# One group of 512-column products per piece of probabilities in an attention stage

## The reference

```python
q = heads(xn @ Wq + bq); k = heads(xn @ Wk + bk); v = heads(xn @ Wv + bv)
q = apply_rope(q); k = apply_rope(k)
scores = jnp.einsum('bhid,bhjd->bhij', q, k) / jnp.sqrt(jnp.float32(D_HEAD))
scores = scores * mask + (1.0 - mask) * -1000000000.0      # mask: lower triangle
probs = jax.nn.softmax(scores, axis=-1)
out = jnp.einsum('bhij,bhjd->bhid', probs, v)
```

## Time and profile before

| | |
|---|---|
| median of timed runs | 3622.78 us |
| profiled execution, span of all instructions | 3621.2 us |
| `phase2`, first weighted sum to last | 835 to 2786 us |
| TensorE busy, whole span | 3255.9 us (90%) |
| VectorE / ScalarE / GpSimd busy | 2606.9 / 1734.9 / 928.2 us |
| TensorE idle ahead of each pass of the loop | 2.99 us |
| L1048 (weighted sum), instructions | 11264, 772.9 us busy |
| L1020 (products for exp) | 3072, 905.5 us busy |
| L1003 (products for max) | 3072, 937.9 us busy |

### The profile page before, as it was taken

How to read it: one execution, slowest core, us unless ns; L and a number is a source line. 1 busy time by engine, 2 the same in 40 slices (tenths; PEclk the granted TensorE clock), 3 DMA queues, 4 the chain that set the end, 5 groups by cost and what they waited for, 6 DMA issues and landing times. The chain is left out here.

```text
span 3621.2 us, 79826 instructions
## 1 busy us (share of the span) xinstructions
PE 3255.9 (90%) x22839; PEld 1559.7 (43%) x22839; DVE 2606.9 (72%) x7405; ACT 1734.9 (48%) x3559; POOL 928.2 (26%) x1205
## 2 busy tenths in 40 slices
PE   2888888859999999999999999999998998499999
PEld 1444444413333333333333333333333776265788
DVE  5999999958888888888888888888882555300232
ACT  1444444415767666766766676667666111011000
POOL 4888877721111111111111111111111000201000
PEclk7999989968999999999999999999999999699999
DMA  2566566582434334444344343334442665412000
GB/s 91 156 186 176 171 180 191 167 181 50 95 83 95 80 87 91 91 91 91 91 91 87 85 92 85 82 87 91 91 91 86 232 256 214 150 63 88 3 11 11
DMA packets 173071, 401.91 MB, mean 111 GB/s; under 512 B 34141, under 2 KB 84611, under 8 KB 155927
## 3 DMA queue, kind: packets, MB, share of 16 engines
q1 hardware_dynamic: 152664, 358.73, 37.6%
q10 hardware_dynamic: 18432, 33.56, 2.9%
q0 software_dynamic: 1536, 4.33, 0.4%
HBM read 239.61 MB, written 156.98 MB: 110 GB/s over the span
## 5 line engine op out<-in xcount | busy, mean ns | idle before, releaser
L969 ACT ACTIVATE prob<-ps 128x512 f32<-128x512 f32 (+1 forms) x2560 | 1282.1, 553 | 673.9 <-PE ps L1020 655.0
L892 DVE CUSTOM_DVE_ANT_0 junk<-ps,mask 128x128 bf16<-128x128 f32 (+3 forms) x2048 | 942.5, 486 | 305.5 <-PE ps L1003 285.7
L1003 PE MATMUL ps<-k_rows,q_rows 96*128 96x512 bf16 (+3 forms) x3072 | 937.9, 337 | 78.5 <-DVE mx L892 37.2
L1020 PE MATMUL ps<-q_rows,k_rows 99*128 99x512 bf16 (+3 forms) x3072 | 905.5, 335 | 42.1 <-issue 38.2
L1048 PE MATMUL ps<-prob,v_rows 128*32 128x256 f32 (+1 forms) x11264 | 772.9, 355 | 0.0
L871 POOL TENSOR_SCALAR_AFFINE_SELECT prob<-prob 128x512 f32<-128x512 f32 x512 | 321.8, 640 | 1684.4 <-ACT prob L969 1684.2
L889 DVE TENSOR_REDUCE mx<-ps 128x1 f32<-128x512 f32 x1024 | 687.1, 686 | 41.1 <-PE ps L1003 28.9
L1020 PEld LDWEIGHTS ps<-q_rows,k_rows 99*128 99x128 bf16 x3072 | 275.1, 98 | 600.1 <-ACT prob L969 354.1
L687 PE MATMUL ps<-w_all,x_t 128*128 128x512 f32 (+1 forms) x1024 | 428.6, 543 | 0.0
L1048 PEld LDWEIGHTS ps<-prob,v_rows 128*32 128x32 f32 x11264 | 232.6, 109 | 448.3 <-issue 373.5
L1003 PEld LDWEIGHTS ps<-k_rows,q_rows 96*128 96x128 bf16 x3072 | 298.0, 99 | 267.9 <-DVE mx L892 82.0
(11 more groups left out here) (126 smaller groups left out, 2821.0 us busy)
## 6 DMA issues: line engine op xcount, KB each, us to landing
k_rows<-k_parts SPq DMA_DIRECT2D x384, 128.0 KB, 6.9
v_ones<-v_st SPq DMA_DIRECT2D x64, 512.0 KB, 8.5
v_rows<-v_ones SPq DMA_DIRECT2D x64, 512.0 KB, 8.9
att<-o_sb ACTq DMA_DIRECT2D x128, 256.0 KB, 5.2
att_b<-att SPq DMA_DIRECT2D x16, 2048.0 KB, 9.6
q_parts<-stage SPq DMA_DIRECT2D x192, 128.0 KB, 2.3
k_parts<-stage SPq DMA_DIRECT2D x192, 128.0 KB, 2.4
q_rows<-q_parts SPq DMA_DIRECT2D x64, 384.0 KB, 4.8
```

What stands on the lines that cost most here:

```text
L892: ins = dve.tensor_tensor_reduce(junk[:, at - PS_A, 0:w], src, mask[:, 512 - w:512], 1.0, MASKED, ALU.add, ALU.max, mx[:, g % 2, h, i:i + 1])
L969: nc.scalar.activation(prob[:, (g * NPC + i) % RING, h, 0:w], src, ACT.Exp).then_inc(exp_done, 1)
L1003: pe.matmul(ps[:, chunk_bank(g, c), 0:w], q[0:ROWS, g, h, i * P:(i + 1) * P], k[0:ROWS, g, h, k0:k0 + w], start=True, stop=True).then_inc( ...
L1020: ins = pe.matmul(ps[:, PS_B + bank(g, n), at:at + w], k[0:AUG, g, h, j * P:(j + 1) * P], q[0:AUG, g, h, q0:q0 + w], start=True, stop=True)
```

## The change

`weigh` loses its argument `part` and runs a whole piece: for each block of the piece (one of 512 or 256 columns, or two of 384 and 128) the four heads, with products as wide as the block. It is called once per piece, after the fourth head's products, where the second half was before. Its waits (`v_in`, `o_copied`, `exp_done`, `sel_done`) stand at its start; they stood at the start of the first half, after head 1. `pv_done` is raised at its end, as before. Pieces, lag, banks, rings and all other engines are unchanged. L1048 has 6144 instructions where it had 11264.

```diff
--- before.py
+++ after.py
@@ -1021,36 +1021,26 @@
                                     q[0:AUG, g, h, q0:q0 + w], start=True, stop=True)
                 ins.then_inc(b_ready, 1)
 
-            def weigh(un, i, part):
+            def weigh(un, i):
 
                 b, g, u = un
                 c, blocks = PIECES[i]
-                if part == 0:
-                    if i == 0:
-                        pe.wait_ge(v_in[g], b * DMA + DMA)
-                        reuse(pe, o_copied, u * 2 - 1)
-                    if i == HALF0:
-                        reuse(pe, o_copied, u * 2)
-                    pe.wait_ge(exp_done, u * NEXP + (i + 1) * HG)
-                    if diag(PIECES[i]):
-                        pe.wait_ge(sel_done, u * NSEL + cut(PIECES[:i + 1]))
-
-                if len(blocks) == 2:
-                    todo = [blocks[0][:1] + blocks[0][1:3] + (256,)] if part == 0 else \
-                        [(blocks[0][0], 256, blocks[0][2] + 256, 128), blocks[1]]
-                else:
-                    j, at, q0, w = blocks[0]
-                    todo = [(j, at + part * w // 2, q0 + part * w // 2, w // 2)]
-                for j, at, q0, w in todo:
+                if i == 0:
+                    pe.wait_ge(v_in[g], b * DMA + DMA)
+                    reuse(pe, o_copied, u * 2 - 1)
+                if i == HALF0:
+                    reuse(pe, o_copied, u * 2)
+                pe.wait_ge(exp_done, u * NEXP + (i + 1) * HG)
+                if diag(PIECES[i]):
+                    pe.wait_ge(sel_done, u * NSEL + cut(PIECES[:i + 1]))
+                for j, at, q0, w in blocks:
                     for h in range(HG):
                         col = q0 - c * HALF
-
                         ins = pe.matmul(ps[32 * h:32 * h + 32, PS_O + c, col:col + w], v[:, g, j, h, :],
                                         prob[:, (g * NPC + i) % RING, h, at:at + w],
-                                        start=(i in (0, HALF0) and part == 0),
-                                        stop=(i in (HALF0 - 1, NPC - 1)), skip_group_check=True)
-                if part == 1:
-                    ins.then_inc(pv_done, 1)
+                                        start=(i in (0, HALF0)), stop=(i in (HALF0 - 1, NPC - 1)),
+                                        skip_group_check=True)
+                ins.then_inc(pv_done, 1)
 
             def prologue():
                 for n in range(AHEAD):
@@ -1075,10 +1065,10 @@
                             scores_for_max(ahead, c)
                         if ahead is None and g == NG - AHEAD and (i, h) == (1, 0):
                             turn_max(unit(LAST, NG - 1), last=True)
-                        if h % 2 and i >= LAG:
-                            weigh(un, i - LAG, h // 2)
-                        elif h % 2 and not first:
-                            weigh(before(un), NPC + i - LAG, h // 2)
+                    if i >= LAG:
+                        weigh(un, i - LAG)
+                    elif not first:
+                        weigh(before(un), NPC + i - LAG)
 
             prologue()
             for n in range(NG):
@@ -1089,8 +1079,7 @@
             for n in range(NG):
                 step(unit(LAST, n), unit(LAST, n + AHEAD) if n + AHEAD < NG else None)
             for i in range(NPC - LAG, NPC):
-                for part in range(2):
-                    weigh(unit(LAST, NG - 1), i, part)
+                weigh(unit(LAST, NG - 1), i)
```

## The result

The changed kernel takes 3642.45 us (median of four, 3641.14 to 3645.75) beside 3622.33 us for the kernel before on the same chip (3620.80 to 3622.93): ratio 1.0059, 95% interval 1.0045 to 1.0073. That is 20 us slower. 3632 was forecast, with 3592 to 3670 as range and slower as the likeliest side. The profiled execution has a span of 3639.6 us against 3621.2.

What follows compares the result with a forecast made beforehand. TensorE was taken to bound `phase2`, coupled to VectorE through three banks. 62 units x 0.22 (+14), 15 x -0.38 (-6) and +2 made +10 on 3621.2 us, given as 3632 us, range 3592 to 3670.

Steps and rivals of the forecast that it cites:

- What the merge saves: In TensorE's weighted sum, one whole group for two halves saves 0.235 us in each of 640 pieces, 150 us without added waits.
- Rival 3: A whole 512-column group costs 1.14 us and not 1.00: +45, 3677 us; chance 0.15 together with the clock rival, Rival 2.
- The layout: Over a unit's ten pieces, waits, nearly all for banks, return all of 2.35 us saved: +0.22 us per unit; chance 0.63.
- piece 6: The fourth exp product waits for ScalarE's exponential after its output copy: +0.17 to +0.25 us, taken as +0.20.
- Piece 0 and piece 5: Two pieces of a unit where no bank is late, so each keeps the full saving of -0.235 us.
- Piece 2: VectorE, behind from four `negate` steps, frees the first chunk's bank 1.34 us in; the fourth chunk waits: +0.20 us.
- The distance with the unit boundary: Once in four units the first chunk waits for the unit before; that wait falls from 0.65 to 0.27 us: -0.38.
- Rivals 1: The added bank waits are half as long, 1.28 us per unit, so part of the saving remains: 3556 us; chance 0.18.
- rival 4: The full saving with no wait added: 3472 us; chance 0.04.
- Rival 2: Stops bring the clock in `phase2` down to 0.93: +50, 3680 us; chance 0.15 together with Rival 3.
- the rule of the Trainium skill: Short TensorE idles from cycling PSUM banks can make the clock fall back repeatedly, so the added stops could too.
- The markers: Signs in the profile: TensorE's waits for VectorE grow from 0.5 to some 2.3 us per unit; wrong if under 1.5.

Runs made afterwards that it cites:

- spread_after: The changed kernel with chunks laid out by hand for each of the ten pieces, and the transposed maximum one chunk later: 3465.15 us, ratio 0.9559.
- spread_before: The kernel before (two half groups) with the same hand-laid spread of chunks: 3602.04 us, ratio 0.9937.
- short_after: The changed kernel with VectorE reading only 64 columns of each chunk for its maximum: 3458.32 us, ratio 0.9550.
- short_before: The kernel before with VectorE reading only 64 columns of each chunk for its maximum: 3543.40 us, ratio 0.9786.
- order_after: The changed kernel with the chunks of a piece in another order and the transposed maximum two chunks later: 3556.07 us, ratio 0.9819.
- defer_after: The changed kernel with ScalarE issuing the store of a copied output bank one piece later: 3621.46 us, ratio 0.9994.
- halves_at_end: The kernel before with both half groups run back to back after the last head's products: 3639.81 us, ratio 1.0049.
- after: The changed kernel itself, with one whole group per piece, against the kernel before: 3642.45 us, ratio 1.0059.

## Why the prediction was right

**What the merge saves.** Right. The whole group was put at 1.00 us by a slope; it takes 1.00. `spread_after` against `spread_before` shows 137 of the 150 us once little gives it back. Rival 3 (1.14 us) is out.

**What gives it back.** Right in place and nearly in size. The layout named pieces 1, 2, 3, 4, 6, 7 and 9, and the trace has the stops there. Lengths forecast and measured: piece 1 3.64 and 3.64; piece 3 2.97 and 2.97, with its last chunk at 1.67 and 1.66; piece 6 3.22 to 3.30 and 3.22; piece 9 3.27 and 3.27 (1909.01 to 1912.28), its fifth chunk at 1.96 and 1.95. That VectorE's hand-over of banks is the main cause is shown by `short_after` against `short_before`, that it is the order and not its load by `order_after` and `spread_after`, and what ScalarE's copy and store cost in piece 6 by `defer_after`.

**The sum, where it was short.** Forecast +0.22 us per unit, measured +0.45. Three terms of the layout were too small, by 0.25 together (piece 6 was 0.03 too large):
- Piece 0 and piece 5 were taken as free, -0.235 each. They are -0.12 and -0.19 (2.83 to 2.71, 2.88 to 2.69). Their fourth exp product now comes so early, as these pieces have one chunk less, that it waits for the first one's bank, a wait that the forecast looked for in piece 6 and in the last two units only. Its rule there (0.43 + 0.65 = 1.08 into the piece at the least) would have given almost nothing, for unhindered the product would come at 1.05 and 1.10. It starts at 1.16 and 1.15, because the first exponential starts 0.51 and 0.50 after its product here (1912.28 to 1912.79 in piece 0) and not 0.43.
- Piece 2 was put at +0.20 and is +0.29. Its fourth chunk starts 1.43 into the piece, not 1.34. VectorE's last `negate` step ahead of it (L920) takes 0.69 us where it took 0.56, in nearly every unit. The forecast had the step at its old length. The traces show what goes with it: GpSimd's L871 runs at that time, two instructions of 0.64 us. Before, L920 starts 0.21 us into the first of them and ends 0.13 behind it; afterwards it starts 0.68 in, in the second, and ends 0.14 behind that one. The merge shifted the two engines against each other.

```profile
1888.27 1.22 POOL L871 TENSOR_SCALAR_AFFINE_SELECT prob<-prob 128x512 f32<-128x512 f32 x2 [2.72 <-ACT prob L969]
1888.95 0.68 DVE L920 TENSOR_TENSOR m<-m_rest,m 32x128 bf16<-32x128 f32 x1
1889.56 0.54 DVE L892 CUSTOM_DVE_ANT_0 junk<-ps,mask 128x384 bf16<-128x384 f32 x1
```

The same in the kernel before:

```profile
1882.45 1.27 POOL L871 TENSOR_SCALAR_AFFINE_SELECT prob<-prob 128x512 f32<-128x512 f32 x2 [2.81 <-ACT prob L969]
1882.66 0.55 DVE L920 TENSOR_TENSOR m<-m_rest,m 32x128 bf16<-32x128 f32 x1
```

- The distance with the unit boundary was put at 0.22 - 0.38 = -0.16 and is -0.06. The chunk's own wait fell as laid out: it starts 0.49 into piece 0 (0.88 before). Under that wait ScalarE's in piece 0 is hidden, so of the missing 0.23 only 0.10 shows.

Over 62 units the missing 0.23 is 14 us; what the longer distance and the passes of the loop (+0.38 and not +0.45) take off is some 3 us. In the piece at half clock behind a pass (1820.58 to 1824.77 in the changed kernel) TensorE shows no stop for a bank, which fits that; it was not tried. The rest nearly cancels: 0.8 us more than forecast behind the last transposed maximum, 1.5 less ahead of the first. That is the 10 us between 3632 and 3642. So the mechanism was right and its size was short by half; that the number came so near is in small part luck, by the waits of piece 0 that lie under another wait once in four units and by the 1.5 us.

**The rivals.** Rivals 1 (waits half as long) and 4 (full saving) are out here; the merge comes near rival 4 under another order (137 of 150 us). Rival 2, the clock: the profile refutes it as the main cause. `phase2` has 0.98 as before, 0.97 in its last stretch. 235 stops for VectorE up to 0.7 us long left the granted clock within 0.01 of where it was. By that, the rule of the Trainium skill that stood against the change (TensorE: Matmul & The Clock Gate, "A second HAM failure mode: psum-queue depth-cycling") does not apply to stops of this size here. One thing stays open. Around each pass of the loop, where TensorE stands for some 3 us, the granted clock is 0.5 (1.2 of 2.4 GHz) for 3.4 or 6.8 us. Over the 13 passes this came to 58 us in the kernel before and to 75 us in the changed one. The same pass in the two, the kernel before first; a mean of 0.79 over these 8 us is 3.4 us at half, one of 0.57 is 6.8:

```profile
1192.00:1200.00 8.00, 5.93 (x48) 2.36 (x48) 3.25 (x14) 3.36 (x6) 0.63 (x1) 0.79 0.02 5
```

```profile
1192.00:1200.00 8.00, 6.24 (x31) 2.55 (x31) 2.44 (x9) 2.94 (x6) 0.64 (x1) 0.57 0.03 7
```

At half speed 17 us are worth 8.5 us at most. In `halves_at_end` it came to 61 us, and its profiled span is that of the changed kernel (3639.8 and 3639.6), so little of the loss hangs on it. Whether the small part that may be left is of the change or of where the passes happen to fall was not settled. Of the distances above only that with the pass contains it.

**The markers.** The waits for VectorE by the table were to grow to 2.3 us per unit and grew to 1.6 (95.5 us in some 60 units, about 4 in a unit where 8 were forecast), close to the 1.5 below which the layout was to count as wrong. The table counts from the end of a product and so shows short stops not at all; by starts the unit above has the 8, in pieces 1, 2, 3, 4, 7 and 9.

## What to carry to other kernels

A saving on the bounding engine can be worth nothing while its order of issue stays laid out for the old lengths. After taking a pause out of the middle, ask for each producer step which buffer it needs, and when the consumer frees it. Here the same merge cost 20 us, or brought 137, by the order of equal instructions alone. Busy shares do not show this: VectorE at 81% held TensorE up for 95.5 us by the table, and at 90% in a better order for 14.2.

## What the runs showed of the hardware

- Float32 products on four strips of 32 partitions chain without loss: one group of 512 columns (`after`), two of 256 back to back (`halves_at_end`), or 384 and 128 (`after`, 1893.68 to 1894.68), are all 1.00 to 1.01 us. The change between these and the bf16 products costs 0.09 us ahead of the group and, by an estimate from the slope over widths (0.36, 0.57 and 1.00 us for 128, 256 and 512 columns), 0.15 in it.
- VectorE's L920, a 32 x 128 subtraction with the same operands everywhere, takes 0.27 to 0.28 us whenever no GpSimd instruction (L871) runs at its start: in all 64 units of `order_after`, `short_before` and `short_after`. Where one runs, it ends 0.12 to 0.15 us behind the end of a GpSimd instruction (61 of 62 units in the kernel before and in the changed one). So it takes a median of 0.56 us in the kernel before, 0.69 in the changed one and 0.38 in the three runs with the spread order. That the one waits for the other is read from the traces; no run took GpSimd's work away. Part of what the better orders gain, at most 0.4 us a unit, may be this.
- ScalarE starts an exponential of 512 columns 0.43 us to 0.51 us (1912.28 to 1912.79 in the changed kernel) after its product's start. TensorE's next product for that bank, where it waits, starts 0.65 us after the exponential (1912.79 to 1913.44).
